# Chased scatters of a five-layer graph kernel: a landing is awaited three tiles back instead of a round of four at a time

## The reference, cut to what matters

```
h = relu(layernorm(x)); x = x + relu(segsum(h[src] @ W_rel[type], dst) + h @ W_loop + b)   # REL
h = relu(layernorm(x)); x = x + attention over edges, summed by src                        # ATT
h = relu(layernorm(x))
h1 = relu(LN(h @ Ws0.T + mean_dst(h[src]) @ Wn0.T + b0))                                   # SAGE0
x = x + LN(h1 @ Ws1.T + mean_dst(h1[src]) @ Wn1.T + b1)                                    # SAGE1
h = relu(layernorm(x)); x = x + segsum(norm * (h @ W)[src], dst), with self loops          # GCN
```

## Time and profile before

| | |
|---|---|
| median of three runs | 3975.69 us |
| profiled execution | 3976.37 us, its span 3974.6 us |
| busy share of the span | PE 65%, DVE 62%, POOL 62%, PE weight loads 52%, ACT 44% |
| mean granted clock of TensorE | 0.771 |
| bytes moved by DMA | 638.48 MB, mean 161 GB/s |

### The profile page before, as it was taken

How to read it: one execution, slowest core, us unless ns; L and a number is a source line. 1 busy time by engine, 2 the same in 40 slices (tenths; PEclk the granted TensorE clock), 3 DMA queues, 4 the chain that set the end, 5 groups by cost and what they waited for, 6 DMA issues and landing times.

```text
span 3974.6 us, 66355 instructions
## 1 busy us (share of the span) xinstructions
PE 2580.5 (65%) x14044; PEld 2047.2 (52%) x14044; DVE 2483.4 (62%) x10828; ACT 1729.4 (44%) x4561; POOL 2474.8 (62%) x2378
## 2 busy tenths in 40 slices
PE   5888868884665655000898676566766774666666
PEld 3444446664555554000786555455655664556666
DVE  6777769894554544787666655444566565556666
ACT  2333337774444443011445555311344444555555
POOL 5777736667888887445776555577544445764443
PEclk9999989997777777555667766655788875569989
DMA  7355538883333332897224666522577773226766
GB/s 270 123 194 213 194 131 271 271 265 72 41 41 41 41 41 34 271 313 238 52 52 132 222 222 214 158 52 52 181 237 237 229 244 90 53 57 216 224 220 216
DMA packets 328229, 638.48 MB, mean 161 GB/s; under 512 B 61072, under 2 KB 89776, under 8 KB 321992
## 3 DMA queue, kind: packets, MB, share of 16 engines
q1 hardware_dynamic: 233406, 501.99, 38.2%
q0 software_dynamic: 90944, 133.85, 14.8%
q10 hardware_dynamic: 3786, 1.65, 0.2%
HBM read 371.35 MB, written 277.50 MB: 163 GB/s over the span
## 4 chain that ended last, share of the span: by engine, by line
DMA 19%; POOL 18%; issue 14%; DVE 5%; ACT 2%; PE 1%; POOLq 0%; DVEq 0%; SPq 0%; ACTq 0%
DMA sums<-parked,last_i 14%; POOL sums L764 11%; POOL got L732 7%; DMA got<-rowsg,gidx 3%; DVE out_stats L1691 2%; DMA got<-rows,gidx 1%; PE bank L1163 1%; DVE out_mv L1698 1%; ACT out_sd L1066 1%; ACT e_h L901 1%; DVE n_t L1791 1%; DVE e_stats L1473 0%; DVE den L1783 0%; DMA rows<-ring 0%; DMA ring<-sums 0%
## 5 line engine op out<-in xcount | busy, mean ns | idle before, releaser
L764 POOL DMA_INDIRECT sums<-parked,last_i x588 | 604.5, 1028 | 670.7 <-DMA sums<-parked,last_i 505.9
L732 POOL DMA_INDIRECT got<-rows,gidx x588 | 603.8, 1027 | 213.7 <-issue 167.9
L1027 ACT ACTIVATE n_h<-ring 128x128 f32<-128x128 f32 x1176 | 483.3, 482 | 211.7 <-DVE ring L1747 131.3
L1306 PE MATMUL bank<-ring,ident 128*128 128x128 f32 x2352 | 508.8, 302 | 0.0
L1303 PE MATMUL bank<-w_t,n_ht 128*128 128x128 f32 x1568 | 360.4, 357 | 135.8 <-DMA ring<-sums 135.7
L1173 PE MATMUL bank<-parked 128*128 128x512 f32 x784 | 374.9, 622 | 78.7 <-DVE parked L1565 76.1
L1279 PE MATMUL bank<-ident,n_h 128*128 128x128 f32 x1176 | 225.7, 323 | 303.4 <-ACT n_h L1027 283.0
L1306 PEld LDWEIGHTS bank<-ring,ident 128*128 128x128 f32 x2352 | 410.4, 218 | 0.0
L1163 PE MATMUL bank<-ident,e_h 128*128 128x128 f32 x588 | 137.8, 378 | 400.1 <-ACT e_h L901 399.5
L1303 PEld LDWEIGHTS bank<-w_t,n_ht 128*128 128x128 f32 x1568 | 290.0, 253 | 200.6 <-DMA ring<-sums 163.3
L778 POOL DMA_INDIRECT attsums<-ring,sidx x196 | 312.3, 1593 | 79.7 <-issue 63.5
(11 more groups left out here) (190 smaller groups left out, 6631.9 us busy)
## 6 DMA issues: line engine op xcount, KB each, us to landing
ring<-sums SPq DMA_DIRECT2D x392, 264.0 KB
ring<-rows SPq DMA_DIRECT2D x392, 264.0 KB, 3.7
rows<-ring SPq DMA_DIRECT2D x294, 264.0 KB, 3.8
ring<-attsums SPq DMA_DIRECT2D x98, 264.0 KB
rowsg<-ring SPq DMA_DIRECT2D x98, 264.0 KB, 3.2
ring<-rowsg SPq DMA_DIRECT2D x98, 264.0 KB, 4.8
sums<-parked SPq DMA_DIRECT2D x16, 1584.0 KB
attsums<-parked SPq DMA_DIRECT2D x16, 1584.0 KB
```

Of the source, the lines that this page charges most:

```text
L732: pool.indirect_dma_start(out=got[:, b, j, 0:width], out_offset=None, in_=table[:, :], in_offset=bass.IndirectOffsetOnAxis(ap=gidx[:, b, j ...
L764: pool.indirect_dma_start(out=sums[:, :], out_offset=bass.IndirectOffsetOnAxis(ap=last_i[:, t:t + 1], axis=0), in_=parked[:, t, :], in_off ...
L1027: last = nc.scalar.activation(n_h[:, b, k, :], x_data(phase, g)[:, k, :], ACT.Relu, bias=x_col(phase, g, k, COL_C), scale=x_col(phase, g, ...
L1306: last = nc.tensor.matmul(o, lhsT=ident[:, :], rhs=s_rows(phase, g)[:, k, 0:D], start=False, stop=(bias is None or k == K - 1))
```

## The change

The constant `UNDER_WAY` = 3 and three semaphores `tile_out` are added. The functions `round_landed` and `scatter_parked` of a round are replaced by functions of a tile. Scatter t counts on `tile_out[t % 3]`. Before scatter t (from the fourth on) POOL waits for the landing of scatter t-3, by `tile_landed`, and when that tile was the last of its round it increments `rounds_landed`. After the last scatter POOL waits for the three left. The wait for the parked round stays before the first tile of each round; the gate is passed before each scatter. The semaphores `scattered` are now used by REL alone.

```diff
+    UNDER_WAY = 3
...
+        tile_out = [Signal(sem(f"tile_out{b}"), 16) for b in range(UNDER_WAY)]
...
-                def round_landed(r):
-                    b = r % 2
-                    pool.wait_ge(scattered[b].sem, (parity_first(seg_index(phase), b) + r // 2 + 1) * 16 * TPR)
-                    pool.sem_inc(rounds_landed.sem, 1)
-
-                def scatter_parked(r):
-                    pool.wait_ge(parked_ready.sem, parked_before(phase) + r + 1)
+                def tile_landed(t):
+                    b = t % UNDER_WAY
+                    tiles = TILES // UNDER_WAY + (1 if b < TILES % UNDER_WAY else 0)
+                    pool.wait_ge(tile_out[b].sem, (CHASED.index(phase) * tiles + t // UNDER_WAY + 1) * 16)
+                    if t % TPR == TPR - 1:
+                        pool.sem_inc(rounds_landed.sem, 1)
+
+                def scatter_parked(t):
+                    if t % TPR == 0:
+                        pool.wait_ge(parked_ready.sem, parked_before(phase) + t // TPR + 1)
                     gate(pool)
-                    for j in range(TPR):
-                        t = r * TPR + j
-                        pool.indirect_dma_start(
-                            out=sums[:, :], out_offset=bass.IndirectOffsetOnAxis(ap=last_i[:, t:t + 1], axis=0),
-                            in_=parked[:, t, :], in_offset=None,
-                            bounds_check=bound, oob_is_err=False).then_inc(scattered[r % 2].sem, 16)
+                    pool.indirect_dma_start(
+                        out=sums[:, :], out_offset=bass.IndirectOffsetOnAxis(ap=last_i[:, t:t + 1], axis=0),
+                        in_=parked[:, t, :], in_offset=None,
+                        bounds_check=bound, oob_is_err=False).then_inc(tile_out[t % UNDER_WAY].sem, 16)
...
-                    for r in range(ROUNDS):
-                        scatter_parked(r)
-                        round_landed(r)
+                    for t in range(TILES):
+                        if t >= UNDER_WAY:
+                            tile_landed(t - UNDER_WAY)
+                        scatter_parked(t)
+                    for t in range(TILES - UNDER_WAY, TILES):
+                        tile_landed(t)
```

## The result

The kernel after takes 3742.56 us (median of four runs, 3740.57 to 3744.57) against 3976.90 us for the kernel before in the same session (3972.27 to 3983.72): a ratio of 0.9409, interval 0.9393 to 0.9426, 234 us less. The forecast was 3776 us, range 3710 to 3900. Lines have moved by a few: L767 is the chased scatter, L637 the load of `sums`, L761 POOL's increment of `rounds_landed`, and L431 the increment that the text calls the gate.

What follows compares the result with a forecast made beforehand. The scatter loop was taken to bound all three stretches, leaving a hole per round. Gains of 67 + 73 + 75 = 215 us, less 5 us per stage end, net 200: 3976 - 200 = 3776 us, range 3710 to 3900.

Steps and rivals of the forecast that it cites:

- Rival D: No change: the node stage, not the scatter loop, holds the pace after all; chance 5%.
- the shift to PE or to freed slots: Sign: SyncE's waits at the load of `sums` move in part from POOL's queue to PE or freed slots.
- The law: Scatter loop: four scatters take the larger of 5.1 us issue and (L + 0.90) x 4/3, with node-stage floors.
- L: Time from a chased scatter's start to its landing; taken as 4.0 us in SAGE0 and GCN, 5.1 in SAGE1.
- SAGE0's PE term: PE's floor for a SAGE0 round: 5.8 us, or 6.7 if the granted clock fell to 0.62; 6.7 taken.
- REL's share of 0.88: DMA busy share of REL's node stage, used as floor: rounds of 6.4 us in SAGE0 and GCN, 8.1 in SAGE1.
- The 15 us for the ends: Node stages end with more queued: each of three stage ends grows by 5 us, cutting 215 us to 200.
- The restart: From a landing to the start of the scatter waiting for it on POOL: 0.90 us, charged to every scatter.
- one idle gap each: Sign: each chased scatter has one idle gap, about 0.6 us in GCN and 1.0 in SAGE1, mostly ended by a landing.
- case A: Lower floor: L stays 3.4 us or node stages reach DMA share 0.95; 317 us gained, 3660 us; chance 10%.
- B: Small gain: L rises to 5.1 us everywhere, 6.16 in SAGE1, 3947 us; milder form 3846 us; chance 22%.
- Case C: Slower: landings slow until three in flight carry less than a drained round of four; 4082 us; chance 6%.

Runs made afterwards that it cites:

- depth 4: The kernel after with UNDER_WAY = 4 instead of 3, so four scatters under way: 3615.25 us, 0.9104 of the kernel before.

## Why the prediction was right

*The pace setter.* That the scatter loop sets the pace of all three stages held: depth alone moved every period, from 8.4 to 5.1 us in GCN, and the idle time that left POOL (242.5 us) covers the time gained. Rival D is out by this too. SyncE's waits for POOL at the load of `sums` fell from 1231.7 to 964.0 us, but those for PE stayed (169.9 and 172.8 us): the shift to PE or to freed slots that I had named as a sign did not come, for with three under way the scatter loop still held the pace.

*The law and L.* The round was to take (L + 0.90) x 4/3. The periods after give L = 4.05 us in SAGE0 and 4.04 in GCN, where I took 4.0, and 4.8 in SAGE1, where I took 5.1. The trace confirms it without the law: the landings that the chain of the kernel after passes in the three scatter stretches (49, 55 and 47 of them) took 4.07, 4.81 and 4.06 us on the mean. That L would rise with the load was reasoned. That it would be 4.0 was a choice between 3.4 and 5.1, and that it fitted within 0.1 us is partly luck. The share of 0.86 in SAGE0 and GCN is in the range I named; SAGE1's 0.93 is above it. GCN came to 6.58 us for 6.55, SAGE0 to 6.60 for 6.7. The clock did not fall as feared for SAGE0's PE term; it rose to 0.89.

*The mis-sized term.* SAGE1's round of 8.2 us stood on two figures. The one of the DMA engines, 8.1 us at REL's share of 0.88, was taken as a floor and was none: after the change the share was 0.93, with depth 4 1.00, and a round took 7.58 and 6.37 us. The other, L = 5.1, was misread from the period. I had charged three issue steps with 3 x 1.27 = 3.81 us, but in SAGE1 they took 4.28 on the mean of 48 rounds, and the step from the fourth scatter to the next first one 5.50, so that L today was 4.6 us and not 5.1. The chain has the same: 48 landings, 4.59 us on the mean. L did not stay at its value of today, as I had assumed, but rose from 4.6 to 4.8; 5.1 came near it because reading it too high made up for leaving out its growth, and that is luck. 48 x (8.2 - 7.58) = 30 us, and they are most of the 33 us by which the forecast fell short. SAGE0 gained 5 us more than forecast, since its round was bound by L and not by PE's 6.7 us. The 15 us for the ends were 10.5; the other 5.4 us, a later start of SAGE0 and gather stages, were in no term.

*The cost of the new instructions.* The restart was charged at 0.90 us for every scatter. That is what it takes behind both increments; behind the gate alone the chain has 0.81 us, and where a landing came just in time it is less. With the landings of the chain the law at 0.90 gives rounds of 6.6, 7.6 and 6.6 us, as measured, so the charge was right or slightly high. That waits and gates that are met cost nothing held (alone, all gaps 0.30 us). That a gate behind a blocking wait could be left out for 35 us I had not seen; it was in the formula, as part of the 0.90. The sign "one idle gap each" came only in part: some 120 of 196 scatters of a stage start more than 0.35 us after the one before has ended, and the mean gap over all is 0.73 us.

*The rivals.* L neither stayed at 3.4 us (the first form of case A) nor rose to 5.1 everywhere (B); it went to 4.1 and 4.8. Of the two levels weighed ahead, the Trainium skill's page DMA: Bandwidth & Descriptors, in its section on the anatomy of one DMA, calls the fixed part of about 2.0 us constant: the 2.23 us of a scatter alone agree with it, the 4.1 and 4.8 beside the row loads do not. The same page's section on latency and other measured facts has HBM access at 2 us at high load; the estimate of 4.0 us made from it is what SAGE0 and GCN show, and SAGE1 is above it. Case C, a landing so slow that three in flight carry less than a round with a drain, did not come. The kernel with two under way is slower than before, but by its depth: its landings are short, 3.3 us, and (3.3 + 0.9) x 2 = 8.4 us is above 8.1. Case A's rounds of 5.9, 6.0 and 7.5 us, at a DMA share of 0.95, are passed by depth 4.

*What stays open.* Why L rises with the load, whether by shared packets in the engines or by slower writes at the memory, no run separates. Nor does one show why the issue steps in SAGE1 are longer than 1.27 us.

## What to carry to other kernels

Where one queue issues, drains and issues again, write the round as issue + restart + landing, and ask how many must be in flight before the landing is no longer on the way: n x step > L + restart, with the L under the load that the change will bring, not today's. Read L from the landings themselves and the steps from the timeline; a period minus assumed steps puts the error of the steps into L. A floor read from another stage's busy share is a floor only if a run has shown that stage to be limited by it. Halving the bytes tells, and so does holding one stage back until the other is done, which shows what each takes alone. Take some more depth than the law asks for, since L grows with what it lets through; here eight under way were 7 us better than four.

## What the runs showed that I had not expected

- A semaphore increment, whichever, between a wait that blocks and an indirect DMA: 0.77 us from the increment to the start of the scatter, where 0.27 us passed from the landing without one. Taking the gate from three of four scatters gave 35 us of 3742, and nothing where the waits are met.
- The busy share of the DMA engines comes near 1.0, and passes it, before the throughput stops rising: 312 GB/s at 0.97 (with half of one operand left out), 348 at 1.01, 379 at 1.04, in one and the same stage.
- The register read from SBUF on SyncE's queue takes 0.79 us (median of 66), longer than two of its DMA issues of 0.33 to 0.39 us, and became the limit of a stage once everything else had been hidden.
